# Cross-attention of a two-part layer rebuilt: half-array scores, merged value products, late softmax division, unrolled steps

## The chip, the cores and the metric

The kernel runs on one core of a Trainium2 chip. The metric is the device time of one execution in microseconds (us). The core has four compute engines that run their own instruction streams: PE (TensorE, matrix products; its weight loads are listed as PEld), DVE (VectorE), ACT (ScalarE) and POOL (GpSimd). SP (SyncE) only issues transfers. The streams wait for each other through semaphores.

## The reference

```python
x = x + xattn(layernorm(x), ctx, ctx, gamma)      # x, ctx: (4, 512, 512)
x = x + ffn(layernorm(x))
# xattn: 8 heads of 64 rows per batch, queries = rows of layernorm(x)
qk  = einsum('bhdq,bhdl->bhql', qh, kh) / sqrt(64)
ret = einsum('bhql,bhdl->bhdq', softmax(qk), vh)   # keys and values are both ctx
# ffn: shared part silu(x @ sw_gate) * (x @ sw_up) @ sw_down, times sigmoid(x @ shared_gate_w),
#      plus the two best of 8 experts of each row, by softmax(x @ router_w.T)
```

Everything is float32. The kernel reaches that precision by splitting each operand into a rounded high part and the low rest, and by adding the products high x high, high x low and low x high.

## The kernel before

The 2048 rows of x are 16 tiles of 128 rows; a tile holds two heads of 64 rows, called s = 0 and s = 1. The kernel has three stages: attention with the second norm and the router's logits, tile by tile; the shared part of the FFN, for four blocks of 512 rows and eleven weight chunks; and the routed experts, 39 slots of 128 rows. Only the first stage and its two ends are touched.

For one tile the attention stage does this. SP loads the tile of x twice (`xb` for the norm, `x2b` for the residual), the context rows once as `cn` for the values and once more, by half tiles, as `cd`, in which each head's 64 rows stand in both halves of the partitions. DVE takes the moments of `xb`, POOL the power -1/2 (`power`), ACT writes the normed queries `xn`. A query stationary `qs` holds, for one head, the high part in 64 partitions and the low part in the other 64 (ACT `queries_hi`, POOL `queries_lo`). POOL splits the keys into `kh` and `kl` (128x1024 each). PE's `scores` makes a 128x512 block of scores with two matmuls over all 128 rows (L1231, L1232), eight blocks a tile. DVE takes the negative row maximum (L922), ACT the exponential with its row sum (L679), DVE the reciprocal, POOL divides the block (`norm_p`, L548). PE transposes the probabilities (`probs_T`, L1239, 4 transposes of 128x128 into one bank), ACT copies the high part (`probs_hi`, L685), DVE subtracts for the low part (`probs_lo`, L931), and PE multiplies with the values in three matmuls of 512 columns (`times_v`, L1252, L1253, L1255) into `bO`. DVE's `rows_out` (L937) adds gamma times `bO` to `x2b`. Then follow the second norm (`moments`, `power`, ACT `normed`, giving `x2n`), a transposition (`rows_T`), its copy `x2T`, and `logits`. SP stores `x2b`, `x2n` and `x2T`.

The order of each engine's stream is written by hand in five functions `tile(t, i, par)`, run by `over_tiles` (L284): two pairs of tiles unrolled, a hardware loop, the last pair unrolled. Scores of tile t+1 are made between the products of tile t; the second norm of tile t-1 and the logits of t-2 ride along. Four banks hold scores, two (`bT`) transposed probabilities, one (`bO`) the product, one (`bM`) everything else.

At the far end the first two weight chunks of the shared part are split (`weights_hi`, `weights_lo`) within the last tile, and `tokens_hi`, `tokens_lo` split the first block of tokens there. PE runs `gate_up` for chunks 0 and 1 before the first `down`. The load of chunk 2 stands in SP's stream behind `store_columns` of the last tile; the splits of chunks 2 and later stand ahead of the first `hidden_hi` on ACT.

## Time and profile before

| | us |
|---|---|
| median of 3 runs | 939.79 (939.73 to 942.89) |
| the profiled execution | 942.02, span 939.7 |
| granted TensorE clock over the span | 0.980 |
| PE busy | 876.7 (93%) |
| DVE, ACT, POOL busy | 571.4, 518.9, 473.7 |
| attention stage, first instruction to the first matmul of the shared part | 0 to 278.2 |

An engine's busy time is the sum of its instructions' spans. Matmuls overlap each other in these spans, so what one costs is read from start to start. "Idle before, releaser" names what ended an engine's wait. Granted clock 1.00 means 2.4 GHz, 0.5 would be 1.2 GHz.

### The profile page before, as it was taken

What the parts mean: (1) busy time and instruction counts of PE and PEld (TensorE: products, weight loads), DVE (VectorE), ACT (ScalarE), POOL (GpSimd) and SP (SyncE); (2) the same over time, 40 slices, a digit from 0 to 9 for tenths busy, and PEclk for the clock granted to TensorE, in tenths of its full rate; (3) what the DMA queues carried; (4) which work ended last, traced back from release to release, by engine and by line L of the source; (5) the groups of instructions that cost most, each with busy time, mean ns of one, the idle gap of its engine ahead of it and who ended that gap; (6) DMA issues with size and microseconds to landing.
All of it is one profiled execution on the core that took longest, in us unless ns stands there. A gap on an engine that the chain in (4) does not pass through costs nothing.

```text
span 939.7 us, 14497 instructions
## 1 busy us (share of the span) xinstructions
PE 876.7 (93%) x4560; PEld 748.0 (80%) x4560; DVE 571.4 (61%) x920; ACT 518.9 (55%) x879; POOL 473.7 (50%) x460
## 2 busy tenths in 40 slices
PE   4899999899988999998899999999999999999993
PEld 3677777787767888886688888888899999999992
DVE  5788787878773642431121212112899999999892
ACT  4788888888765331120111211112688888888881
POOL 5787878787720000047100000000489999999984
PEclk9999999999999999999799999999999999999997
DMA  9344343525625322200032002552964444443542
GB/s 145 83 142 128 127 142 101 160 96 156 224 90 157 100 68 90 90 1 1 1 120 39 1 1 90 185 184 93 300 145 72 87 70 80 76 87 67 90 63 39
DMA packets 70142, 93.77 MB, mean 100 GB/s; under 512 B 16137, under 2 KB 35593, under 8 KB 70098
## 3 DMA queue, kind: packets, MB, share of 16 engines
q1 hardware_dynamic: 60338, 72.73, 25.9%
q0 software_dynamic: 9760, 20.49, 12.3%
q8 instruction: 24, 0.39, 0.2%
q14 instruction: 20, 0.16, 0.1%
HBM read 65.59 MB, written 27.60 MB: 99 GB/s over the span
## 4 chain that ended last, share of the span: by engine, by line
PE 68%; ACT 1%; issue 1%; DVE 1%; DMA 0%; POOLq 0%; SPq 0%; POOL 0%; DVEq 0%; ACTq 0%
PE bank L1347 9%; PE bank L1345 8%; PE bank L1346 8%; PE bank L1412 5%; PE bank L1414 5%; PE bank L1413 5%; PE bank L1359 4%; PE bank L1360 4%; PE bank L1361 4%; PE bank L1436 3%; PE bank L1437 3%; PE bank L1438 3%; PE bank L1369 2%; PE bank L1423 1%; DMA stg<-in_L_ffn_sw_down 0%
## 5 line engine op out<-in xcount | busy, mean ns | idle before, releaser
L1033 DVE TENSOR_TENSOR sg<-bank,sg 128x512 f32<-128x512 f32 x44 | 30.4, 692 | 224.0 <-PE bank L1347 187.5
L606 POOL DMA_INDIRECT xg<-x_normed_rows,meta x39 | 39.7, 1018 | 219.3 <-PE bank L1369 159.7
L1347 PE MATMUL bank<-x_hl,wsp 128*128 128x512 f32 x352 | 138.5, 393 | 5.2 <-issue 5.1
L1346 PE MATMUL bank<-x_hl,wsp 128*128 128x512 f32 x352 | 138.1, 392 | 2.3 <-issue 2.3
L1345 PE MATMUL bank<-x_hl,wsp 128*128 128x512 f32 x352 | 138.3, 393 | 0.7 <-issue 0.6
L785 ACT ACTIVATE sg<-bank 128x512 f32<-128x512 f32 x44 | 26.3, 597 | 164.9 <-PE bank L1347 147.8
L591 POOL DMA_INDIRECT slot_rows<-msrc,posi x32 | 32.9, 1030 | 135.9 <-DVE posi L1140 126.5
L685 ACT ACTIVATE pth<-bank 128x512 fp32r<-128x512 f32 x128 | 73.3, 598 | 45.8 <-PE bank L1239 43.9
L931 DVE TENSOR_TENSOR ptl<-bank,pth 128x512 fp32r<-128x512 f32 x128 | 86.0, 682 | 17.6 <-ACT pth L685 17.2
L792 ACT ACTIVATE hh<-sg 128x512 fp32r<-128x512 f32 x44 | 27.8, 631 | 123.7 <-DVE sg L1033 107.9
L548 POOL TENSOR_SCALAR pb<-pb,rinv 128x512 f32<-128x512 f32 x128 | 87.4, 696 | 13.3 <-DVE rinv L927 7.8
L679 ACT ACTIVATE pb<-bank,negmax 128x512 f32<-128x512 f32 x128 | 86.7, 688 | 0.7 <-DVE negmax L922 0.3
L922 DVE TENSOR_REDUCE negmax<-bank 128x1 f32<-128x512 f32 x128 | 81.9, 681 | 0.7 <-PE bank L1232 0.2
L1347 PEld LDWEIGHTS bank<-x_hl,wsp 128*128 128x128 f32 x352 | 66.7, 189 | 19.2 <-issue 5.4
L1345 PEld LDWEIGHTS bank<-x_hl,wsp 128*128 128x128 f32 x352 | 66.7, 189 | 17.6 <-issue 4.0
L617 POOL DMA_INDIRECT out<-y,meta x39 | 73.5, 1885 | 12.3 <-issue 5.5
L1346 PEld LDWEIGHTS bank<-x_hl,wsp 128*128 128x128 f32 x352 | 66.7, 190 | 15.2 <-issue 1.6
L1231 PE MATMUL bank<-kh,qs 128*128 128x512 f32 x128 | 57.7, 451 | 20.5 <-POOL qs L531 17.2
L627 POOL TENSOR_TENSOR wd<-wex,wd 96x512 fp32r<-96x512 f32 x39 | 74.5, 1911 | 3.3
L1239 PE MATMUL bank<-ident,pb 128*128 128x128 f32 x512 | 71.9, 273 | 4.2 <-POOL pb L548 4.2
L1239 PEld LDWEIGHTS bank<-ident,pb 128*128 128x128 f32 x512 | 61.3, 141 | 15.6 <-POOL pb L548 5.3
L1359 PE MATMUL bank<-wsp,hh 128*128 128x512 f32 x176 | 69.6, 395 | 2.9 <-DVE hl L1035 2.4
(157 smaller groups left out, 2353.9 us busy)
## 6 DMA issues: line engine op xcount, KB each, us to landing
cd<-in_ctx SPq DMA_DIRECT2D x32, 256.0 KB, 5.0
wex<-in_L_ffn_w_gate SPq DMA_DIRECT2D x8, 704.0 KB, 4.3
wex<-in_L_ffn_w_up SPq DMA_DIRECT2D x8, 704.0 KB, 5.7
xb<-in_x SPq DMA_DIRECT2D x16, 256.0 KB, 4.5
cn<-in_ctx SPq DMA_DIRECT2D x16, 256.0 KB, 3.0
x2b<-in_x SPq DMA_DIRECT2D x16, 256.0 KB, 2.8
x_rows<-x2b SPq DMA_DIRECT2D x16, 256.0 KB, 2.1
x_normed_rows<-x2n SPq DMA_DIRECT2D x16, 256.0 KB, 2.0
```

Source lines behind the costliest of these rows:

```text
L548: gp.tensor_scalar(pb[s][:, q, :], pb[s][:, q, :], rinv[:, s, q:q + 1], 0.0, ALU.mult, ALU.add).then_inc(g_pn, 1)
L617: g.indirect_dma_start(out=out, out_offset=bass.IndirectOffsetOnAxis(ap=meta[:, s, 0:1], axis=0), in_=y3[s % 2][:, :], in_offset=None, com ...
L627: gp.tensor_tensor(wd3[0:IR, 1, c], wex[0:IR, e, 2 * W3 + (IC - 1) * H:EW], wd3[0:IR, 0, c].bitcast(F32), ALU.subtract).then_inc(g_wd, 1)
L679: sc.activation(pb[s][:, q, :], bS[q][:, :], ACT.Exp, bias=negmax[:, s, q:q + 1], scale=1.0, accum_out=rsum[:, s, q:q + 1]).then_inc(a_exp, 1)
L685: sc.activation(pth[c][:, :], bT[c % 2][:, :], ACT.Copy).then_inc(a_pth, 1)
L922: ve.tensor_reduce(negmax[:, s, q:q + 1], bS[q][:, :], AX_X, ALU.max, negate=True).then_inc(d_max, 1)
L931: ve.tensor_tensor(ptl[c][:, :], bT[c % 2][:, :], pth[c][:, :].bitcast(F32), ALU.subtract).then_inc(d_ptl, 1)
L1239: ins = te.transpose(bT[c % 2][:, q * P:(q + 1) * P], pb[s][:, q, c * P:(c + 1) * P], ident[:, :])
L1345: te.matmul(bk[:, :], hi, xhi, start=(h == 0), stop=False)
L1346: te.matmul(bk[:, :], hi, xlo, start=False, stop=False)
L1347: ins = te.matmul(bk[:, :], lo, xhi, start=False, stop=(h == HC - 1))
L1359: te.matmul(bY[tt][:, :], th, hi, start=(c == 0), stop=False)
```

## The change

The work is the same up to the order of the operations. These parts change:

1. Loads: `cd` is gone; keys and values both come from `cn` (`load_keys` removed, one 256 KB load a tile where there were three).
2. Scores: `qh`, `ql`, `kh`, `kl` are 128x512 with one head in each half of the partitions. For each of the four 128-query chunks of a tile PE issues six matmuls of 64 rows by 512 columns, alternating between the halves of the array and between two banks. DVE takes the maxima of both heads of a chunk in one instruction of 2x512 elements.
3. Values: the stationary of a head is its 64 high and 64 low columns side by side, so the product with `pth` and with `ptl` takes two matmuls, not three, and leaves the high and the low contribution in the two halves of `bO`. ACT copies one half (`low_half`), DVE adds it to the other (`halves`), once a head.
4. The softmax division leaves `norm_p`. One reciprocal of eight sums a tile, spread by POOL to 128x512 (`spread`), transposed by PE (`inverses`), copied by ACT times gamma (`rgam`), multiplied into the product by POOL (`scaled`), and added to `x2b` by POOL (`residual`).
5. POOL now writes `xn`, `qh` and `x2n`; ACT's `normed` and `queries_hi` are gone.
6. Transposed probabilities rotate over three banks (`bT`, order `P_BANK`); the third also takes what `bM` took.
7. `over_tiles` runs `step(i)` for i from -3 to 20, fully unrolled. Step i has scores 1 to 3 of tile i and score 0 of tile i+1, transposes of tile i-1 (and the first of tile i), products of tiles i-1 and i-2, norm of tile i-3. On PE `gate_up(0, 0)` stands after step 16 and `gate_up(0, 1)` after step 17. SP issues in step i: `store_rows(i-4)`, `load_x2(i-2)`, `store_columns(i-5)`, `store_normed(i-5)`, `load_x(i+3)`, `load_values(i+1)`.

The core of the diff:

```diff
-        cd = [place(f"cd{j}", [P, 2, L]) for j in range(2)]
-        kh = [place(f"kh{j}", [P, 2, L], F32R) for j in range(2)]
-        qs = [place(f"qs{j}", [P, L], F32R) for j in range(2)]
-        vs = [place(f"vs{j}", [P, 2, LC, 3, DH], F32R) for j in range(2)]
+        kh = [place(f"kh{j}", [P, L], F32R) for j in range(2)]
+        qh = [place(f"qh{j}", [P, L], F32R) for j in range(2)]
+        vs = [place(f"vs{j}", [P, LC, 4, DH], F32R) for j in range(2)]
...
-        bS, bT, bO, bM = bank[0:4], bank[4:6], bank[6], bank[7]
+        bO, bT = bank[4], bank[5:8]
+        P_BANK = (2, 0, 2, 0, 2, 0, 1, 0)
...
+            def load_values(t):
+                after(sp, e_vt, t - 1)
                 after(sp, kl_done, t - 1)
+                sp.dma_start(cn[t % 2][:, :], c_t[t, :, :]).then_inc(ld_cn[t % 2], 16)
+
+            def load_x2(t):
+                after(sp, g_x2n, t - 1)
+                after(sp, st_x2[t % 2], 16 * (t // 2))
+                sp.dma_start(x2b[t % 2][:, :], x_t[t, :, :]).then_inc(ld_x2[t % 2], 16)
...
+            def spread(t):
+
+                g.wait_ge(d_rinv, t + 1)
+                after(g, e_R, t)
+                gp.tensor_copy(rspr[:, :, :], rinv[:, :, :].rearrange("p c s -> p (c s)").unsqueeze(2).to_broadcast([P, 2 * QC, DH])).then_inc(g_rspr, 1)
+
+            def scaled(t):
+
+                g.wait_ge(d_att, 2 * t + 2)
+                g.wait_ge(a_Rg, t + 1)
+                gp.tensor_tensor(att[t % 2][:, :], att[t % 2][:, :], rgam[:, :], ALU.mult).then_inc(g_att, 1)
...
+            def step(i):
+                if there(i + 1):
+                    keys_hi(i + 1)
+                    queries_lo(i + 1)
+                if there(i - 2):
+                    scaled(i - 2)
+                if there(i + 1):
+                    keys_lo(i + 1)
...
+                    shift(0, i + 2)
+                    queries(i + 2)
+                if there(i - 3):
+                    shift(1, i - 3)
+                if there(i + 2):
+                    queries_hi(i + 2)
+                if there(i - 3):
+                    rows_normed(i - 3)
+                if there(i - 2):
+                    residual(i - 2)
...
+                after(pe, a_exp, 8 * t + 2 * c - 2)
+                terms = ((qh, kh), (qh, kl), (ql, kh))
+                for n, (a, b) in enumerate(terms):
+                    for s in range(2):
+                        r = slice(DH * s, DH * (s + 1))
+                        ins = te.matmul(bSS[c % 2][:, s, :], a[t % 2][r, c * P:(c + 1) * P], b[t % 2][r, :], start=(n == 0), stop=(n == 2))
+                        if n == 2:
+                            ins.then_inc(e_s, 1)
...
-                te.matmul(bO[:, :], hi, pth[c][:, :], start=first, stop=False)
-                te.matmul(bO[:, :], lo, pth[c][:, :], start=False, stop=False)
-                pe.wait_ge(d_ptl, 4 * k + c + 1)
-                te.matmul(bO[:, :], hi, ptl[c][:, :], start=False, stop=last).then_inc(e_pv, 1)
...
+                te.matmul(bO[:, :], v, pth[n % 4][:, :], start=(c == 0), stop=False)
+                pe.wait_ge(d_ptl, 8 * t + n + 1)
+                te.matmul(bO[:, :], v, ptl[n % 4][:, :], start=False, stop=(c == LC - 1)).then_inc(e_pv, 1)
```

SP's stream, the transfers of one tile. First before (rows of the hardware loop; `cd` are the key halves, `st_`, `ld_` semaphores count landed transfers, `a_`, `d_`, `g_`, `e_` those of ACT, DVE, POOL, PE):

```order
L362 DMA x_normed_transposed<-x2T_100 128x512 [waits a_x2T]
L356 DMA x_rows<-x2b_95 128x512
L358 DMA x_normed_rows<-x2n_97 128x512 [waits a_x2n]
L352 DMA x2b_95<-in_x 128x512 [waits st_x20,a_x2n]
L344 DMA cn_72<-in_ctx 128x512 [waits e_vt]
```

And the same place in the change, one step:

```order
L351 DMA x_rows<-x2b_102 128x512 [waits g_x2]
L347 DMA x2b_102<-in_x 128x512 [waits st_x21,g_x2n]
L359 DMA x_normed_transposed<-x2T_105 128x512 [waits a_x2T]
L355 DMA x_normed_rows<-x2n_103 128x512 [waits g_x2n]
L337 DMA xb_69<-in_x 128x512 [waits d_stat0,g_xn]
L342 DMA cn_71<-in_ctx 128x512 [waits kl_done,e_vt]
```

The context load `cn`, of which the keys are now made as well, stands behind the load of `x2b`, which waits for POOL's `g_x2n`; before, the keys came by the loads `cd`, ahead of the stores.

POOL's stream in the change, one step (`att` is the product, `rgam` the spread inverse sums):

```order
L531 CAST kh_74<-cn_72 128x512 [waits e_s,ld_cn1]
L525 TENSOR_TENSOR ql_80<-xn,qh_78 128x512 [waits g_qh]
L554 TENSOR_TENSOR att_97<-att_97,rgam 128x512 [waits a_Rg,d_att]
L535 TENSOR_TENSOR kl_76<-cn_72,kh_74 128x512 [waits g_kh]
L504 TENSOR_TENSOR rstd<-vare,mhalf 128x1 [waits d_vare1]
L548 COPY rspr<-rinv 128x512 [waits e_R,d_rinv]
L504 TENSOR_TENSOR rstd<-vare,mhalf 128x1 [waits d_vare0]
L508 TENSOR_SCALAR nmr<-aggr,rstd 128x1 [waits g_rstd0]
L514 TENSOR_SCALAR xn<-xb_69,rstd,nmr 128x512 [waits g_nmr0]
L508 TENSOR_SCALAR nmr<-aggr,rstd 128x1 [waits g_rstd1]
L520 CAST qh_77<-xn 128x512 [waits e_s,g_xn]
L542 TENSOR_SCALAR x2n_104<-x2b_102,rstd,nmr 128x512 [waits e_x2T,st_x2n1,g_nmr1]
```

Eight divisions a tile have left this stream; three passes over the product, the normed rows and the spread sums have come in. The first row of a step waits for `cn`, and its last one here sets `g_x2n`.

PE's stream around one chunk of scores, before and in the change:

```order
L1239 MATMUL bank<-ident,pb_86 128x128 x3
L1231 MATMUL bank<-kh_75,qs_82 128x512 [waits a_exp]
L1232 MATMUL bank<-kl_77,qs_82 128x512
L1231 MATMUL bank<-kh_75,qs_82 128x512
L1232 MATMUL bank<-kl_77,qs_82 128x512
L1252 MATMUL bank<-pth_89,vs_84 128x512 [waits a_pth]
```

```order
L1214 MATMUL bank<-ident,pb_87 128x128 x3
L1205 MATMUL scores<-kh_74,qh_78 128x512 [waits a_exp,kl_done,ql_done]
L1205 MATMUL scores<-kh_74,qh_78 128x512
L1205 MATMUL scores<-kl_76,qh_78 128x512 x2
L1205 MATMUL scores<-kh_74,ql_80 128x512 x2
L1214 MATMUL bank<-ident,pb_87 128x128 [waits d_ptl]
```

Four matmuls for two score blocks became six for two blocks, each of half the rows; the wait for the keys (`kl_done`) sits on the first chunk of each tile.

## Rows read from the trace of the kernel before

**Rows 1.** One line, L937, the end of each tile (length ns, first and last start us)

```profile
L937 DVE SCALAR_TENSOR_TENSOR x2b<-bank,gam,x2b x16: 742/742/746, 39.5 to 278.6; 128x512 f32<-128x512 f32 x16
```

**Rows 2.** Busy us (x instructions) from 100 to 220: PE, PEld, DVE, ACT, POOL; PEclk, DMA

```profile
100.00:220.00 120.00, 109.98 (x651) 92.15 (x650) 97.32 (x210) 100.25 (x231) 94.53 (x118) 1.00 0.42 136
```

**Rows 3.** The timeline of PE, 15 to 17 us (start, length, instruction)

```profile
15.83 0.40 PE L1231 MATMUL bank<-kh,qs 128*128 128x512 f32 x1
16.07 0.39 PE L1232 MATMUL bank<-kl,qs 128*128 128x512 f32 x1
16.38 0.41 PE L1290 MATMUL bank<-ident,rg 9*128 9x9 f32 x4
16.72 0.50 PE L1231 MATMUL bank<-kh,qs 128*128 128x512 f32 x1
```

**Rows 4.** The timeline of PE, 123 to 127 us

```profile
123.80 0.95 PE L1279 MATMUL bank<-rgT,x2T 128*128 128x9 f32 x8
124.61 0.48 PE L1252 MATMUL bank<-pth,vs 128*128 128x512 f32 x1
...
126.07 1.03 PE L1239 MATMUL bank<-ident,pb 128*128 128x128 f32 x8
126.86 0.48 PE L1231 MATMUL bank<-kh,qs 128*128 128x512 f32 x1
```

**Rows 5.** The timeline of DVE, 121 to 124 us

```profile
121.53 1.25 DVE L922 TENSOR_REDUCE negmax<-bank 128x1 f32<-128x512 f32 x2
...
122.77 0.68 DVE L931 TENSOR_TENSOR ptl<-bank,pth 128x512 fp32r<-128x512 f32 x1
123.36 0.68 DVE L894 BATCH_NORM_STATS2 stats<-xb 128x6 f32<-128x512 f32 x1
```

**Rows 6.** The timeline of SP, the first and fifth transfer of a burst

```profile
65.37 0.33 SPq L358 DMA_DIRECT2D x_normed_rows<-x2n  x1
...
67.20 1.25 SPq L340 DMA_DIRECT2D cd<-in_ctx  x2
```

**Rows 7.** DMA issues from 145 to 153 us, a burst of six (last column: us to landing)

```profile
cd<-in_ctx SPq DMA_DIRECT2D x2, 256.0 KB, 4.3
...
cn<-in_ctx SPq DMA_DIRECT2D x1, 256.0 KB, 3.0
```

**Rows 8.** One line, L625, a cast on POOL (length min/median/max)

```profile
L625 POOL CAST wd<-wex x39: 601/1312/2017, 661.2 to 921.5; 96x512 fp32r x38, 96x512 fp32r<-96x512 f32 x1
```

**Rows 9.** Groups of instructions on POOL, 100 to 220 us (busy, mean ns, idle before)

```profile
L548 POOL TENSOR_SCALAR pb<-pb,rinv 128x512 f32<-128x512 f32 x60 | 41.0, 698 | 4.1 <-POOL qs L531 4.1
...
L542 POOL TENSOR_TENSOR kl<-cd,kh 128x1024 fp32r<-128x1024 f32 x7 | 16.8, 2399 | 0.0
...
L519 POOL TENSOR_TENSOR rstd<-vare,mhalf 128x1 f32<-128x1 f32 x14 | 7.7, 552 | 1.5 <-issue 1.5
L521 POOL TENSOR_SCALAR nmr<-aggr,rstd 128x1 f32<-128x1 f32 x14 | 3.7, 265 | 2.4 <-POOL rstd L519 2.4
```

**Rows 10.** The timeline of all engines at the start

```profile
8.77 7.43 SPq L335 DMA_DIRECT2D xb<-in_x  x1
...
20.62 1.35 PE L1239 MATMUL bank<-ident,pb 128*128 128x128 f32 x8 [2.70 <-POOL pb L548]
```

**Rows 11.** The timeline of all engines, 262 to 285 us

```profile
262.77 1.03 PE L1239 MATMUL bank<-ident,pb 128*128 128x128 f32 x8
...
267.52 1.91 ACT L714 ACTIVATE x_hl<-x_hl 128x2048 fp32r<-128x2048 f32 x1
...
269.46 2.29 DVE L972 TENSOR_TENSOR x_hl<-x_hl 128x2048 fp32r<-128x2048 f32 x1 [1.11 <-ACT x_hl L714]
...
274.63 1.75 DVE L966 TENSOR_TENSOR wsp<-stg,wsp 128x1536 fp32r<-128x1536 f32 x1
...
284.97 0.33 SPq L362 DMA_DIRECT2D x_normed_transposed<-x2T  x1
```

**Rows 12.** The timeline of PE at 294 us

```profile
294.01 0.47 PE L1359 MATMUL bank<-wsp,hh 128*128 128x512 f32 x1 [2.36 <-DVE hl L1035]
```

More of the change, by code:

```diff
@@ L1020, in _, with step @@
-            over_tiles(dve, tile)
-            rows_out(NT - 1, NI - 1, 1)
-            dve.wait_ge(d_x2, NT)
-            moments(1, NT - 1, x2b[1][:, :])
-            aggregate(1, NT - 1)
-            variance(1, NT - 1)
+            def step(i):
+                if there(i - 1):
+                    inverse(i - 1)
+                if there(i - 2):
+                    probs_lo(i - 2, 7)
+                if i == 1:
+                    router_columns()
+                if there(i - 1):
+                    values_lo(i - 1)
+                if there(i + 2):
+                    aggregate(0, i + 2)
+                if there(i - 1):
+                    probs_lo(i - 1, 0)
+                if there(i + 2):
+                    variance(0, i + 2)
+                if i == NT:
+                    weights_lo(0)
+                if there(i):
+                    maxima(i, 1)
+                if there(i - 1):
+                    probs_lo(i - 1, 1)
+                if there(i - 2):
+                    halves(i - 2, 1)
+                if there(i - 1):
+                    probs_lo(i - 1, 2)
+                if there(i - 3):
+                    second_norm(i - 3)
+                if there(i - 1):
+                    probs_lo(i - 1, 3)
+                if there(i - 3):
+                    aggregate(1, i - 3)
+                if i == NT:
+                    weights_lo(1)
+                if there(i):
+                    maxima(i, 2)
+                if there(i - 3):
+                    variance(1, i - 3)
+                if there(i - 1):
+                    probs_lo(i - 1, 4)
+                if there(i + 3):
+                    first_norm(i + 3)
+                if there(i):
+                    maxima(i, 3)
+                if there(i - 1):
+                    probs_lo(i - 1, 5)
+                    halves(i - 1, 0)
+                    probs_lo(i - 1, 6)
+                if i == NT - 1:
+                    tokens_lo(0, 0)
+                if there(i + 1):
+                    maxima(i + 1, 0)
@@ L1392, in block2 @@
                     rows3(1, 0, 1)
-            logits(NT - 2, 0)
+            for i in range(-3, NT + 1):
+                step(i)
             gate_up(0, 0, 0)
-            rows_T(NT - 1, 1)
-            logits(NT - 1, 1)
+            step(NT + 1)
+            gate_up(0, 1, 0)
+            for i in range(NT + 2, NT + 5):
+                step(i)
             for b in range(NB):
```

713 lines of the change are left out of this document (309 added, 404 removed).

## The prediction

> **What bounds the kernel now.** I read the page's slices first: PE is busy in nearly all of them, and only the first 278 us hold the work that changes. The end of a tile, L937, comes 16 times from 39.5 to 278.6 us, so a tile takes 239.1 / 15 = 15.94 us [rows 1]. Per tile the engines are busy, from 120 us in the middle [rows 2], PE 14.6, ACT 13.3, DVE 12.9, POOL 12.6 us. PE is nearest to the period, at clock 1.00 (2.4 GHz), and the missing 1.3 us are waits. What it does, from start to start: a matmul of 512 columns 0.24 us, alone or behind its like [rows 3]; the eight passes of the logits 0.81 us [rows 4]. Forty matmuls and ten blocks of four transposes then leave (14.6 - 40 x 0.235 - 0.8) / 10 = 0.44 us for a block; the bare spacing of eight is 0.79 us [rows 4].
>
> **PE after the change.** Values: 16 instead of 24 matmuls, 3.8 us. Eleven blocks of transposes (one is new, the inverse sums): 4.8. Logits: 0.8. Scores: 24 matmuls of half the rows. If the two of a pair run beside each other, 12 x 0.235 = 2.8 us; if not, 5.6. No row shows a 64-row matmul. They use different halves of the array and write different banks, and the weight loads that they need, one per matmul, are no more than what PE takes in transposes every 0.10 us [rows 4]; I take 2.8 and keep 5.6 as the other end. Four times a step PE goes into such a group and out again. The nearest row is the nine-row transposes: 16.07 to 16.38 us is 0.07 more than the usual 0.24 [rows 3], so eight changes cost up to 0.6 us. Sum: 12.8 us, against 14.6; the other end is 15.0 to 15.6.
>
> The Trainium skill, "TensorEngine Tiling (Array Packing)", Key Properties, says that tiles work in parallel but that a change of tiling mode drains the engine. By that rule, with a drain as the 0.16 us by which a matmul's length exceeds its spacing (0.39 against 0.235), the eight changes would cost 1.3 us and PE would stand at 13.5; the row shows half of that. Neither sum reaches the loop below; the rule would only lift rival B.
>
> **DVE.** A 512-wide pass costs 0.59 us, two maxima and a variance 1.24 [rows 5]. Four double maxima at 1.12 (a second 512 elements without a second start), eight `probs_lo`, the value split, two moments, two `halves` and 0.4 for small ones: 4.5 + 4.7 + 0.6 + 1.2 + 1.2 + 0.4 = 12.6 us. It hardly changes. **ACT** loses four passes (`xn`, `x2n`, two of `queries_hi`) and gets three; it stays under DVE. Reading the four streams beside each other with these lengths, every wait among PE, ACT and DVE closes within about 13.0 us, so DVE would set the pace.
>
> **POOL and SP: a new loop.** This is what I expect to decide. In step i SP may issue `load_x2(i-2)` only when POOL has finished `rows_normed(i-4)`; two stores, `xb`, and then `cn` stand behind it in SP's stream. `keys_hi`, POOL's first instruction of step i, waits for that `cn`, and `rows_normed(i-3)` is POOL's last but one in the same step. So one step closes one round: from the end of `x2n` to the issue of `cn`, its landing, and POOL's stream up to the next `x2n`. Before, the keys' loads were not behind `x2n` of the same round, since `cd` was issued a tile earlier.
> - Issue: the fifth transfer of a burst starts 1.83 us after the first [rows 6], plus 0.1 to wake.
> - Landing: 3.0 us for the third transfer of a burst, 4.3 for the fifth and sixth [rows 7]. Ours is the fifth of smaller ones: 3.8, bounds 3.0 and 4.3.
> - POOL: a cast of 512 at 0.57 (0.60 long at its shortest [rows 8]), three times with `spread`; three two-input passes at half of the 1024-wide 2.4 [rows 9], 3.6; two powers 1.1; two shifts 0.54, two waits on its own results at 2.4 / 14 = 0.17; a scaling at 0.67 and one at 0.70 [rows 9]. Sum 1.71 + 3.6 + 1.1 + 0.54 + 0.34 + 1.37 = 8.7 us. `residual` falls into the transfer's time.
>
> Together 1.9 + 3.8 + 8.7 = **14.4 us a step** (13.6 to 14.9), above 12.8 and 13.0. The saving of PE's 1.8 us is thus mostly handed back as a wait for the keys at `scores(i+1, 0)`, and nothing of it depends on PE's exact sum below 14.4.
>
> **The beginning.** PE's first transposes of probabilities start at 20.62 us now [rows 10]. In the change SP issues `cn` of tile 0 only behind `load_x(2)`, which waits for `queries(0)` on POOL, an estimate of 6.4 us. `cn` of tile 1 stands behind the table of slot rows, behind which SP's next issue now takes 7.43 us, from 8.77 to 16.2 [rows 10]. So it is issued at 17, lands at 20.5, and with cast, low queries and low keys (3.0) the scores of tile 1 start at 24; PE's stream has them ahead of the first transposes, which come at 26.4 us: 6 us later than now. Steps 1 to 3 do not close the loop yet and lack some products: 37.5 us, step 4 begins at 64. The keys of step 4 are ready 9.4 into it (`x2n(0)` ends 0.5 before it, then 1.9 + 3.8, a cast and three two-input passes), ten rounds of 14.4 follow, and 2.7 us of PE work: step 15 begins at 64 + 9.4 + 144 + 2.7 = 220.
>
> **The far end.** Now PE goes from the transposes of tile 15 at 262.77 to its first `down` at 294.01 us [rows 11, 12]: 31.2 us. In the change the chain is longer. From the start of step 15: 11 until `probs_lo(14, 6)`, 1.7 for the transposed values and two copies, 1.9 for `tokens_hi` (267.52), 2.3 for `tokens_lo` (269.46) on DVE, for which `probs_lo(14, 7)` and all behind it wait; then DVE, ACT and PE alternate through step 16 with two weight splits on each of ACT and DVE, 1.75 a piece there (274.63), inside it [rows 11]: the last product before `gate_up(0, 0)` ends 33.8 us after the start of step 15. `gate_up(0, 0)` is 24 x 0.235 = 5.6; the three products left 1.4. Then one dependent chain: half copied 0.7, `halves` 0.7, `scaled` 1.2, POOL's norm of tile 14 1.9, `residual` 1.25, moments to variance 1.2, power and shift 1.0, `x2n` 0.8, transposes and copy 1.3, and some hops: 10.9 us, where `x2b` to `x2T` took 6.4 before. From the store of the last `x2T` (284.97) to `down` it is 9.0 us, the load and split of chunk 2 [rows 11, 12]; SP's order there is unchanged. Sum 33.8 + 5.6 + 1.4 + 10.9 + 9.0 = 60.7. `gate_up(0, 1)` is covered. So `down` starts at 220 + 61 = 281 us, 13 us sooner than at 294. Everything behind it is the same program: unchanged, also the unrolled code (2903 listed PE rows against 2694).
>
> **Sum.** The profiled execution took 942.0 us, 2.2 above the median. 942.0 - 13 = 929; against the median 939.8 - 13 = **927 us**.
>
> **Rivals.**
> - B, the loop does not bind. `cn` lands in 3.0 us or the burst has thinned out, and DVE sets 13.0 to 13.3 us. For it: the loop's lower bound is 13.6, and the change moves six transfers of 256 KB a tile where eight are moved now, so that each may land sooner. Then 64 + 11 x 13.2 + 61 = 270, 24 us gained: 916 us.
> - C, slower: the two halves of a pair run one after the other. The nearest rows for it are that every matmul, whatever its rows, starts 0.235 after the last. PE then has 15.3 us a step: 26.4 + 14 x 15.3 - 1.5 + 61 = 300, 6 us later than now: 945.5 us. It decides from 14.9 us a step on, where the longer ends have eaten the gain.
> - D, POOL's passes are longer beside DVE: in the expert stage the cast of L625 takes 1.31 us at the median, 0.60 at its shortest [rows 8]. Against it: in this stage the 1024-wide pass takes a steady 2.40 with DVE busy 97 of 120 us [rows 2, 9], and DVE keeps reading banks. With a fifth more the loop is 16.1: step 15 at 237, `down` at 298, 4 us later than now: 944 us. The Trainium skill, "GPSIMD Engine Reference", Architecture, says that POOL's read and write ports are shared with DVE; by that rule, the long casts are such collisions.
>
> **How the numbers follow.** A measurement can tell about 0.5%, 4.7 us, from no change. My forecast has 0.50, B 0.22, C 0.13, D and mishaps at the ends 0.15. With 4 us of spread on each: faster 0.46 + 0.22 + 0.03 = 0.71; within 0.5% 0.04 + 0.06 + 0.08 = 0.18; slower 0.11. The range reaches from a little below B to C: 913 to 946 us.
>
> **What would show it.** Right: in the middle PE waits at the first scores of each tile for POOL's low keys, POOL waits some 4 us a step for `cn`, and the writes of `x2b` come every 14.4 us; the matmuls of the scores start 0.12 us apart on average; first transposes of probabilities at 26, the first `down` at 281, behind a wait of nearly 9 us. Wrong: PE without waits at 15 us a step (C), POOL passes beyond 1.3 us for 512 elements (D), or DVE without idle time (B). If the loop is right but the start or the end is not, the error shows in those two times alone.

## The result and the profile after

The changed kernel takes 950.23 us (median of 4, 949.24 to 951.39) and the one before, measured between its runs, 941.34 (939.73 to 943.52): ratio 1.0103, 95% interval 1.0078 to 1.0127. It is slower by about 1%, where 927 us (913 to 946) was forecast. Its profiled execution took 949.24, with a span of 947.5 us.

The page after: busy time of the engines, then the granted clock in 40 slices.

```profile
PE 869.6 (92%) x4624; PEld 718.8 (76%) x4624; DVE 569.3 (60%) x820; ACT 507.1 (54%) x863; POOL 428.6 (45%) x414
...
PEclk9899999989877999999799999999999999999997
```

The same stretch as [rows 2], 100 to 220 us, in the changed kernel (the same columns):

```profile
100.00:220.00 120.00, 109.02 (x696) 81.16 (x694) 98.40 (x164) 96.51 (x227) 73.99 (x98) 0.94 0.41 125
```

PE is busy 109.0 of 120 us, as before, although its work of a tile was meant to have shrunk. POOL has 20 us more of idle time, DVE and ACT stand about as before, and the clock has fallen from 1.00 to 0.94. The table of waits, 60 to 220 us (total us, times, longest us):

```profile
POOL kh L531 <- DMA cn<-in_ctx: 53.9, 10, 6.1
...
PE scores L1205 <- issue: 11.0, 7, 2.3
```

The longest wait is the forecast one, POOL's for `cn`: 5.4 us a time. One round of the loop shows in SP's and POOL's timelines:

```profile
129.61 0.33 SPq L347 DMA_DIRECT2D x2b<-in_x  x1
129.99 0.42 SPq L359 DMA_DIRECT2D x_normed_transposed<-x2T  x1
130.46 0.42 SPq L355 DMA_DIRECT2D x_normed_rows<-x2n  x1
130.99 0.43 SPq L337 DMA_DIRECT2D xb<-in_x  x1
131.51 0.41 SPq L342 DMA_DIRECT2D cn<-in_ctx  x1
131.97 0.45 SPq L351 DMA_DIRECT2D x_rows<-x2b  x1
```

```profile
120.91 0.61 POOL L531 CAST kh<-cn 128x512 fp32r<-128x512 f32 x1 [6.08 <-DMA cn<-in_ctx]
...
123.94 1.27 POOL L535 TENSOR_TENSOR kl<-cn,kh 128x512 fp32r<-128x512 f32 x1
...
128.81 0.77 POOL L542 TENSOR_SCALAR x2n<-x2b,rstd,nmr 128x512 f32<-128x512 f32 x1
...
136.84 0.61 POOL L531 CAST kh<-cn 128x512 fp32r<-128x512 f32 x1 [6.00 <-DMA cn<-in_ctx]
```

`x2n` ends at 129.58, `load_x2` leaves at 129.61, and `cn`, fifth of six, 1.9 us behind it at 131.51; the cast of the keys starts at 136.84, 5.3 us later. POOL's part from cast to the end of `x2n` is 8.67 us. From 85.56 to 225.23 us `cn` is issued nine times more, so a step takes 139.67 / 9 = **15.52 us**, not 14.4. What PE makes of it (timeline, before and behind its wait for the keys):

```profile
120.14 0.50 PE L1205 MATMUL scores<-kh,qh 64*128 64x512 f32 x2
120.47 0.40 PE L1205 MATMUL scores<-kl,qh 64*128 64x512 f32 x2
120.71 0.39 PE L1205 MATMUL scores<-kh,ql 64*128 64x512 f32 x2
121.03 0.50 PE L1228 MATMUL bank<-pth,vs 128*128 128x512 f32 x1
```

```profile
125.31 0.80 PE L1205 MATMUL scores<-kh,qh 64*128 64x512 f32 x2 [2.32 <-issue]
125.87 0.66 PE L1205 MATMUL scores<-kl,qh 64*128 64x512 f32 x2
126.30 0.66 PE L1205 MATMUL scores<-kh,ql 64*128 64x512 f32 x2
```

The low keys `kl` are ready at 125.21, and the first scores of the tile start at 125.31: the wait that the profile puts down as "issue" is the one for the keys. Each row of L1205 is two matmuls; a pair takes 0.235 us from start to start, and the spacings around a change of shape are longer, 0.32 or 0.33. Behind the wait of 2.3 us a spacing is 0.43: from 125.3 to 127.0 us the granted clock is 0.50 (1.2 GHz), from 130 us on again 1.00 (2.4 GHz).

### The profile page after: what moved, and what is told of

It reads as the page before. It is cut to its first block, busy times and chain, and to the rows that moved or that the text cites. A ratio compares the mean times of both kernels' runs of the same rounds, so it can differ in the third digit from the quotient of the medians.

```text
span 947.5 us, 13669 instructions
## 1 busy us (share of the span) xinstructions
PE 869.6 (92%) x4624; PEld 718.8 (76%) x4624; DVE 569.3 (60%) x820; ACT 507.1 (54%) x863; POOL 428.6 (45%) x414
## 4 chain that ended last, share of the span: by engine, by line
PE 87%; issue 4%; DMA 3%; DVE 2%; ACT 2%; POOL 1%; SPq 0%; POOLq 0%; DVEq 0%; ACTq 0%
PE scores L1338 9%; PE scores L1337 9%; PE scores L1336 9%; PE bank L1214 6%; PE scores L1205 5%; PE bank L1350 4%; PE bank L1351 4%; PE bank L1352 4%; PE bank L1228 4%; PE bank L1230 3%; PE bank L1432 3%; PE bank L1433 3%; PE bank L1431 3%; PE scores L1407 3%; PE scores L1409 3%
## 5 line engine op out<-in xcount | busy, mean ns | idle before, releaser
L997 DVE TENSOR_TENSOR sg<-scores,sg 128x512 f32<-128x512 f32 x44 | 30.4, 692 | 224.3 <-PE scores L1338 187.5
L1338 PE MATMUL scores<-x_hl,wsp 128*128 128x512 f32 x352 | 139.4, 396 | 3.9 <-issue 3.7
L1337 PE MATMUL scores<-x_hl,wsp 128*128 128x512 f32 x352 | 138.9, 395 | 2.5 <-issue 2.4
L1336 PE MATMUL scores<-x_hl,wsp 128*128 128x512 f32 x352 | 139.3, 396 | 0.1
L768 ACT ACTIVATE sg<-scores 128x512 f32<-128x512 f32 x44 | 26.3, 597 | 165.9 <-PE scores L1338 144.8
L663 ACT ACTIVATE pb<-scores,negmax 128x512 f32<-128x512 f32 x128 | 87.8, 695 | 19.9 <-DVE negmax L905 19.7
L915 DVE TENSOR_TENSOR ptl<-bank,pth 128x512 fp32r<-128x512 f32 x128 | 86.5, 677 | 12.5 <-ACT pth L669 12.2
L1214 PE MATMUL bank<-ident,pb 128*128 128x128 f32 x512 | 83.2, 288 | 9.8 <-DVE ptl L915 9.2
L905 DVE TENSOR_REDUCE negmax<-scores 128x2 f32<-128x1024 f32 x64 | 77.4, 1210 | 20.9 <-PE scores L1205 20.8
L1338 PEld LDWEIGHTS scores<-x_hl,wsp 128*128 128x128 f32 x352 | 67.3, 191 | 22.2 <-issue 8.3
L1337 PEld LDWEIGHTS scores<-x_hl,wsp 128*128 128x128 f32 x352 | 67.4, 192 | 15.6 <-issue 1.8
L1336 PEld LDWEIGHTS scores<-x_hl,wsp 128*128 128x128 f32 x352 | 67.3, 191 | 14.7 <-issue 0.8
L620 POOL DMA_INDIRECT out<-y,meta x39 | 68.2, 1749 | 12.5 <-issue 5.2
L1113 DVE TENSOR_TENSOR wg<-wex,wg 128x1408 fp32r<-128x1408 f32 x39 | 63.4, 1626 | 12.1 <-ACT wg L794 12.1
L1352 PE MATMUL bank<-wsp,hl 128*128 128x512 f32 x176 | 69.4, 395 | 0.0
```

The source lines that it names most:

```text
L620: g.indirect_dma_start(out=out, out_offset=bass.IndirectOffsetOnAxis(ap=meta[:, s, 0:1], axis=0), in_=y3[s % 2][:, :], in_offset=None, com ...
L663: sc.activation(pb[t % 2][s][:, c, :], bSS[c % 2][:, s, :], ACT.Exp, bias=negmax[:, c, s:s + 1], scale=1.0, accum_out=rsum[:, c, s:s + 1]) ...
L905: ve.tensor_reduce(negmax[:, c, :], bSS[c % 2][:, :, :], AX_X, ALU.max, negate=True).then_inc(d_max, 1)
L915: ve.tensor_tensor(ptl[n % 4][:, :], bT[P_BANK[n]][:, :], pth[n % 4][:, :].bitcast(F32), ALU.subtract).then_inc(d_ptl, 1)
L1214: ins = te.transpose(bT[P_BANK[n]][:, q * P:(q + 1) * P], pb[t % 2][s][:, q, c * P:(c + 1) * P], ident[:, :])
L1336: te.matmul(bk[:, :], hi, xhi, start=(h == 0), stop=False)
```

## Three places, each moved by an experiment

The time of the first `down` product tells most of the run: before it came at 294.01 us [rows 12], and 645.7 us of span followed; after it comes at 303.49, and 644.0 follow. So the loss of 8 to 9 us lies in the part that I had summed, and every experiment can be read by that time. The kernels were measured on several chips, each beside the kernel before, which took 927 to 944 us there, so I compare ratios to before; step and first `down` come from each profile. The column of the first transposes scatters: all versions but those with the context early have the same SP stream up to them, and still differ by over 3 us.

| kernel | ratio to before (95%) | step, us | first transposes | first `down` |
|---|---|---|---|---|
| before | 1 | 15.9 | 20.62 | 294.01 |
| after | 1.0103 (1.0078 to 1.0127) | 15.5 | 30.67 | 303.49 |
| loads first | 0.9951 (0.9917 to 0.9986) | 13.62 | 31.39 | 288.88 |
| GpSimd order | 0.9941 (0.9910 to 0.9971) | 13.62 | 32.15 | 288.01 |
| keys twice | 1.0197 (1.0145 to 1.0249) | 16.1 | 35.74 | 314.91 |
| loads first, keys twice | 0.9959 (0.9934 to 0.9984) | 13.62 | 34.54 | 290.05 |
| loads first, `values_lo` twice | 0.9950 (0.9922 to 0.9978) | 13.62 | 34.38 | 290.75 |
| loads first, halves apart | 0.9958 (0.9940 to 0.9976) | 13.63 | 33.72 | 289.64 |
| context early | 1.0082 (1.0049 to 1.0115) | 15.5 | 28.94 | 301.42 |
| context early, slot rows later | 0.9991 (0.9960 to 1.0022) | 15.7 | 21.02 | 296.00 |
| gate and up later | 1.0125 (1.0044 to 1.0206) | 15.6 | 31.79 | 304.99 |
| loads first, splits spread | 0.9888 (0.9834 to 0.9941) | 13.62 | 34.89 | 288.17 |
| and the end rearranged | 0.9770 (0.9738 to 0.9801) | 13.62 | 34.43 | 276.97 |
| all, and the start | 0.9685 (0.9658 to 0.9711) | 13.62 | 22.48 | 265.25 |

### The middle: is the loop the bound?

**Loads first.** `load_x` and `load_values` go to the head of SP's step:

```
             def step(i):
+                if there(i + 3): load_x(i + 3)
+                if there(i + 1): load_values(i + 1)
                 if there(i - 4): store_rows(i - 4)
                 if there(i - 2): load_x2(i - 2)
                 if there(i - 5): store_columns(i - 5); store_normed(i - 5)
-                if there(i + 3): load_x(i + 3)
-                if there(i + 1): load_values(i + 1)
```

> Edit: in each step SP issues load_x and load_values first, then the stores and load_x2 that wait for POOL. Theory (the loop x2n -> load_x2 -> cn -> keys -> x2n sets the period of the changed kernel, 15.5 us a step from the issue of one cn to the next): the loop is cut, the steps come every 13.0 to 13.5 us (DVE is next), POOL no longer waits for cn in the middle, and with some eleven rounds the time falls by 22 to 28 us against the changed kernel, to 922 to 928 us. Rival 1 (the transfers are slow by themselves, the order does not matter): within 3 us of the changed kernel. Rival 2 (PE is the bound, its groups of half-array matmuls cost more than they look): steps stay above 15 us, POOL's waits turn into waits for PE.

Measured: 936.02 us, 14 us under the changed kernel by the ratios. The busy times show what bounds now:

```profile
100.00:220.00 120.00, 120.00 (x815) 89.73 (x814) 112.52 (x189) 111.90 (x264) 86.57 (x113) 1.00 0.44 137
```

PE has not one idle interval, and the clock is 1.00. POOL still waits for `cn`, 29.8 us in 12 rounds instead of 53.9 in 10, but nothing that PE needs waits with it. The gain is less than the 22 to 28 us expected: the step stops at 13.62, not at 13.0 to 13.5, and not eleven rounds get shorter but some nine, since the first wait behind the loop ends 16.7 us sooner (239.19 instead of 255.88). The landing of `cn` also fell, by the table of DMA issues, 60 to 220 us (median us to landing), first after, then here:

```profile
cn<-in_ctx SPq DMA_DIRECT2D x10, 256.0 KB, 4.7
```

```profile
cn<-in_ctx SPq DMA_DIRECT2D x11, 256.0 KB, 2.9
```

So the landing was long in the burst, six transfers within 2.4 us, and is short here, where the loads are spread over the step. The next version stands between them: six transfers within 3.7 us, and 3.7 us to landing.

**GpSimd order.** The second, independent cut leaves SP alone and lets `x2n` end earlier on POOL:

```
                 if there(i + 2): inverse_deviation(0, i + 2)
+                if there(i - 3): shift(1, i - 3); rows_normed(i - 3)
                 if there(i + 2): shift(0, i + 2); queries(i + 2)
-                if there(i - 3): shift(1, i - 3)
                 if there(i + 2): queries_hi(i + 2)
-                if there(i - 3): rows_normed(i - 3)
                 if there(i - 2): residual(i - 2)
```

> Edit: on POOL shift(1) and rows_normed(i-3) stand ahead of the power, shift, queries and queries_hi of tile i+2, so 2.6 us less of POOL's work lies between the arrival of cn and x2n; SP's order is unchanged. Theory (the loop): 15.5 - 2.6 = 12.9, so the DVE takes over at 13.0 to 13.5 us a step and the time falls by 20 to 27 us, about as with SP's order changed, though nothing of the transfers is touched. Rival (the transfers themselves limit, some 6 us of them per step behind one another): the time falls by under 5 us.

Measured: 935.28 us, the step again 13.62. Two edits with nothing in common but the loop give 14 and 15 us.

**Keys twice**, on the changed kernel and on the version with the loads first:

```
+                gp.tensor_copy(kh[t % 2], cn[t % 2]).then_inc(g_kh0, 1)
+                g.wait_ge(g_kh0, t + 1)
                 gp.tensor_copy(kh[t % 2], cn[t % 2]).then_inc(g_kh, 1)
```

> The changed kernel with the cast of the keys done twice on GpSimd (0.6 us more a tile, between the landing of cn and everything behind it). Theory A (the loop x2n, load of x2, two stores, xb, cn, landing, GpSimd work to the next x2n sets the step from step 4 on): eleven rounds longer by 0.6 to 0.7 us each and 1 to 2 us at the start, +8 us, 957 to 960. Rival B (the steps are long because TensorE or VectorE is, or because of transfers in common): GpSimd has 4 us of idle time a step, +1 to +2 us for the start alone, 951 to 952.

> The same doubled cast on top of the version whose loads stand at the head of SyncE's step (936.0). Theory A: there the loop is cut and TensorE sets the step at 13.6 us, GpSimd's waits for cn take up the 0.6 us, only the start gets 1 to 2 us longer: 937 to 938. Rival B (GpSimd's work is still on the path): 8 us more, 944.

Measured: +0.0094 of the ratio on the changed kernel, 8.9 us, and the step from 15.52 to 16.10 by these issues of SP (144.88 us in nine steps); on the other +0.0008, 0.8 us, step 13.62. The same pass costs a step its 0.58 us in the one and nothing in the other. The loop is shown. The first `down` of the slow one moved by 11.4 us, more than the loop gives, because its start is 5.1 us late: 1 us is the doubled pass, the rest the scatter explained under "The start".

```profile
75.88 0.38 SPq L343 DMA_DIRECT2D cn<-in_ctx  x1
...
220.76 0.43 SPq L343 DMA_DIRECT2D cn<-in_ctx  x1
```

**`values_lo` twice**, with the loads first, asks whether PE or DVE stops the step at 13.62:

```
+                ve.tensor_tensor(vs_lo, bT[1], vs_hi, ALU.subtract).then_inc(d_vl0, 1)
+                dve.wait_ge(d_vl0, t + 1)
                 ve.tensor_tensor(vs_lo, bT[1], vs_hi, ALU.subtract).then_inc(d_vl, 1)
```

> The version with the loads first (step 13.62 us), with VectorE's pass for the low part of the values done twice, 0.6 to 0.7 us more of VectorE a step, which is then busy 13.4 of 13.62 us. Theory A: what bounds this version is TensorE, by the spacing of its products (a step between the two shapes of the array costs 0.09 us, and each first product with a new stationary behind another 0.32 instead of 0.235), which makes 13.6 us where the prediction summed 12.8: the step stays within 0.2 us of 13.62, +0 to +3 us in all. Rival B (VectorE's in-order queue is the bound, whatever its gaps): +0.6 to +0.7 us a step, 14.2 to 14.3, +9 to +11 us in all.

```profile
100.00:220.00 120.00, 120.00 (x810) 89.33 (x809) 117.91 (x201) 111.78 (x264) 86.20 (x112) 1.00 0.43 139
```

Measured: DVE goes from 112.5 to 117.9 busy us of 120, and neither step nor ratio moves. VectorE is not the bound, and TensorE, without an idle interval, is. Its timeline (loads first, one group of a chunk):

```profile
124.92 0.47 PE L1228 MATMUL bank<-pth,vs 128*128 128x512 f32 x1
125.23 0.40 PE L1230 MATMUL bank<-ptl,vs 128*128 128x512 f32 x1
125.56 0.50 PE L1205 MATMUL scores<-kh,qh 64*128 64x512 f32 x2
125.89 0.40 PE L1205 MATMUL scores<-kl,qh 64*128 64x512 f32 x2
126.12 0.39 PE L1205 MATMUL scores<-kh,ql 64*128 64x512 f32 x2
126.44 0.50 PE L1228 MATMUL bank<-pth,vs 128*128 128x512 f32 x1
126.78 0.40 PE L1230 MATMUL bank<-ptl,vs 128*128 128x512 f32 x1
```

A change of shape stretches two spacings, not one. Into the group it is 125.23 to 125.89, 0.66 us where two spacings are 0.47; out of it 126.12 to 126.78, again 0.66. Over the eight steps from 97.5 to 206.5 us the 32 entries cost 0.19 us more than the plain spacings on average, the 32 exits 0.17. Eight changes a step are 1.4 us, and that is the difference: 28 products and pairs at 0.235, 44 transposes of 128x128 at 0.109 and eight passes of the logits at 0.112 are 12.3 us, and the step is 13.6. My reading ahead of that run, 0.09 us a change and the rest in the first products of the values, was wrong. Those products do take 0.31 us to the next start behind a block of transposes (124.92 to 125.23), but they start 0.03 us behind the last transpose instead of 0.11, so the sum is the plain one. The kernel before has the same:

```profile
127.18 0.40 PE L1232 MATMUL bank<-kl,qs 128*128 128x512 f32 x1
```

Eight transposes from 126.07 [rows 4] at 0.109 and one product at 0.235 lead to 127.18, though the product starts at 126.86.

### The pairs in the array

**Halves apart**, with the loads first: the three products of one half of the rows, then the three of the other.

```
-                for n, (a, b) in enumerate(terms):
-                    for s in range(2):
+                for s in range(2):
+                    for n, (a, b) in enumerate(terms):
```

> The version with the loads first (936.0, step 13.62 us, TensorE busy without a gap), with the score products of one head's half of the rows issued three in a row, and then those of the other half, instead of in pairs. Theory A: neighbours in the two halves of the array run side by side (two products in 0.235 us), and apart they run one after the other: twelve times 0.235 less one overlap at each of the four changes of half, 1.9 to 2.8 us more a step, 15.5 to 16.4 us, sixteen steps: +28 to +45 us, 964 to 981. Rival C (each product of 64 rows takes half the time by itself, in whatever order): 936 to 938, no change.

Measured: no change, against theory A, but not for rival C's reason either. The timeline of PE:

```profile
124.45 0.51 PE L1205 MATMUL scores<-kh,qh 64*128 64x512 f32 x2
124.79 0.40 PE L1205 MATMUL scores<-kl,qh 64*128 64x512 f32 x2
125.03 0.40 PE L1205 MATMUL scores<-kh,ql 64*128 64x512 f32 x2
```

Starts are recorded, also where ends are modelled. In the program all three products of the first half stand ahead of the second half's first; in the trace both halves' `kh,qh` start before either's `kl,qh`. So the second half's first product started ahead of two that stand before it in the program: here each half of the array worked through its own three products, and the order between the halves did not matter. The Trainium skill, "TensorEngine Tiling (Array Packing)", Key Properties, says that tiles operate independently and can load weights and multiply in parallel; this trace agrees, and adds that adjacency in the program is not needed. It also says that a change of mode drains the engine; here a change costs 0.17 to 0.19 us, close to the 0.16 that I had worked out for that rule, and I had put 0.07 into the sum.

### The start

**Context early**: `cn` of tiles 0 and 1 is loaded right behind `xb` of tiles 0 and 1.

```
+                if i == -2: load_values(0); load_values(1)
-                if there(i + 1):
+                if i > 0 and there(i + 1):
                     load_values(i + 1)
```

> Edit: cn of tiles 0 and 1 is loaded right behind xb of tiles 0 and 1, ahead of the small loads and the table of slot rows. Theory (the late start is the position of these two loads): PE's first transposes of probabilities come at 20 to 22 us instead of 30.7, and the whole time falls by 8 to 10 us against the changed kernel; the middle keeps its 15.5 us a step. Rival (the loop's phase swallows an earlier start, since its first round waits for x2n of tile 0 anyway): the first transposes come earlier, but the time falls by under 3 us.

Measured: 948.75 us, 2 us gained by the ratios, whose intervals overlap, where 8 to 10 were expected. The first transposes came at 28.94 instead of 30.67: something else was late. The table of DMA issues of this run, 0 to 30 us, names it (KB each, median us to landing):

```profile
slot_rows<-meta SPq DMA_DIRECT2D x1, 39.0 KB, 16.8
```

The table of slot rows is 39 KB, but leaves in pieces of 8 bytes and lands 16.8 us later. In the changed kernel `cn` of tile 1, issued at 15.16, stood behind it and POOL waited for it (POOL's timeline):

```profile
24.50 0.62 POOL L531 CAST kh<-cn 128x512 fp32r<-128x512 f32 x1 [9.07 <-DMA cn<-in_ctx]
```

Here `xb` of tile 3, issued at 12.04, landed at 26.2, and VectorE's first pass over it holds the maxima behind it. The landing of the slot rows also explains the scatter of the starts. It took 14.6 us in the changed kernel, and 15.3 to 18.9 in the seven other versions with this start; in all eight the first transposes come 16.0 to 16.3 us behind that time (14.6 and 30.67, 15.3 and 31.39, 18.9 and 34.89), and 17.0 in the two with the keys twice.

**Context early, slot rows later**: the same, and the store moved behind the loads of the dense part's third block.

```
-                sp.dma_start(meta_d..., meta...).then_inc(st_meta0, 16)
...
             load_block(2, 0)
+            sp.wait_ge(g_const, N_CONST)
+            sp.dma_start(meta_d..., meta...).then_inc(st_meta0, 16)
             store_out(0)
```

> The second cut of the start: as in the run with the first two context tiles loaded early, and the store of slot_rows (39 KB in pieces of 8 bytes, 16.8 us from issue to landing there, while xb of tile 2, issued 3.0 us behind it, landed at 26.2 us) moved to the place behind the loads of block 2's columns in the dense part. Theory A: those small pieces stand ahead of every later transfer of the queue, so moving them lets xb and cn through in 3 to 5 us, first transposes of probabilities near 21 us instead of 28.9, and the whole run 7 to 10 us below the changed kernel, 940 to 943. Rival B: the start is set by the chain of norm, scores and exponentials, and the small pieces cost nothing: 948 to 949, as with the early context tiles alone.

Measured: ratio 0.9991, 10.5 us under the changed kernel, first transposes at 21.02. The first `down` moved by 7.5 us, since the loop in the middle is still there. The rest of the run is as long as before (644.4 us behind the first `down`), so the store costs nothing in its new place. The store was not moved by itself.

### The end

**Gate and up later**:

```
-            gate_up(0, 0, 0)
             step(NT + 1)
+            gate_up(0, 0, 0)
             gate_up(0, 1, 0)
```

> Edit: on PE step 17 stands ahead of gate_up(0, 0), not behind it. Theory (gate_up(0, 0), 7.0 us, delays the last three value products and with them the whole chain to the last x2T and to the load of chunk 2): that chain starts 6 to 7 us sooner, both gate_up still lie inside it, and the time falls by 5 to 7 us. Rival (the chain is not what ends the wait of the first down; the weights or tokens are): the time moves by under 2 us.

Measured: nothing gained (ratio 1.0125, interval over that of the changed kernel). The last value product ended earlier, but its successor did not start earlier:

```profile
287.68 0.77 POOL L542 TENSOR_SCALAR x2n<-x2b,rstd,nmr 128x512 f32<-128x512 f32 x1
```

```profile
293.42 0.60 PE L1248 MATMUL bank<-ident,x2n 128*128 128x128 f32 x4
```

The last `x2n`, tile 15's, is ready at 288.45, but its transposes and those of tile 14 ahead of them stand behind `gate_up(0, 1)` until 293.42. In the changed kernel only `gate_up(0, 0)` held this chain up; `gate_up(0, 1)` ran beside the norm of tile 15, whose `x2n` was ready at 292.77, and ended at 292.3. Here both stand in a row between the chain and the last transposes, 5.5 to 7 us each, and what the move gained is lost again. Also untouched are the three waits that come first (the changed kernel's chain of waits):

```profile
252.86 2.29 DVE L936 TENSOR_TENSOR x_hl<-x_hl 128x2048 fp32r<-128x2048 f32 x1 [3.69 <-ACT x_hl L701]
...
261.59 1.76 DVE L930 TENSOR_TENSOR wsp<-stg,wsp 128x1536 fp32r<-128x1536 f32 x1 [4.57 <-ACT wsp L696]
...
271.11 1.76 DVE L930 TENSOR_TENSOR wsp<-stg,wsp 128x1536 fp32r<-128x1536 f32 x1 [4.42 <-ACT wsp L696]
```

DVE stands at a split until ACT has done its half, with `probs_lo` and so PE's next product behind it: PE waits 4.6, 4.5 and 3.1 us and works at half its clock behind each.

**Splits spread**, with the loads first: ACT's high parts stand two or three passes ahead of DVE's low parts, and the last pair a step later.

```
 ScalarE:
-                if i == NT: tokens_hi(0, 0)
                 if there(i): exps(i, 0, 0); exps(i, 0, 1)
...
                 if there(i - 1): probs_hi(i - 1, 2)
-                if i == NT: weights_hi(0)
+                if i == NT: tokens_hi(0, 0)
...
                 if there(i - 1): probs_hi(i - 1, 4); probs_hi(i - 1, 5)
-                if i == NT: weights_hi(1)
+                if i == NT: weights_hi(0)
...
                 if there(i - 1): probs_hi(i - 1, 7)
+                if i == NT + 1: weights_hi(1)
 VectorE:
-                if i == NT: weights_lo(0)
                 if there(i - 1): probs_lo(i - 1, 1)
...
-                if i == NT: weights_lo(1)
                 if there(i - 1): probs_lo(i - 1, 4)
+                if i == NT: tokens_lo(0, 0)
+                if i == NT + 1: weights_lo(1)
                 if there(i - 1): probs_lo(i - 1, 5); halves(i - 1, 0); probs_lo(i - 1, 6)
-                if i == NT - 1: tokens_lo(0, 0)
+                if i == NT: weights_lo(0)
```

> On top of the version with the loads first (936.0): the six passes that split the tokens and the first two weight chunks (ScalarE 1.9, 1.5, 1.5 us, VectorE 2.3, 1.75, 1.75 us) are moved out of the place where each VectorE pass waits for its ScalarE pass ahead of a pass that TensorE needs; they stand two or three passes later on VectorE than on ScalarE, and the last pair a step later. TensorE waited 4.6, 4.5 and 3.1 us for them and ran at half its clock behind each wait. Theory A: most of these 12 us are the in-order wait and go, the passes' own time stays in part: 7 to 11 us less, 925 to 929, the first down product at 278 to 282 instead of 288.9. Rival B: the two engines' work in the steps 16 and 17 is the bound whatever its order, or the end is set by the last stores and the load of the third chunk: 934 to 936.

```profile
244.43 0.66 PE L1214 MATMUL bank<-ident,pb 128*128 128x128 f32 x4 [1.16 <-DVE ptl L915]
...
248.65 0.66 PE L1214 MATMUL bank<-ident,pb 128*128 128x128 f32 x4 [1.40 <-DVE ptl L915]
...
252.00 0.77 PE L1336 MATMUL scores<-x_hl,wsp 128*128 128x512 f32 x1 [2.02 <-DVE wsp L930]
...
268.75 0.79 PE L1336 MATMUL scores<-x_hl,wsp 128*128 128x512 f32 x1 [4.54 <-DVE wsp L930]
...
288.17 0.76 PE L1350 MATMUL bank<-wsp,hh 128*128 128x512 f32 x1 [7.38 <-DVE hl L999]
```

Measured: the three waits fell from 12.2 to 1.2 + 1.4 + 2.0 us, and the last value product came at 260.96, about 7 us sooner. But the second gate and up product now waits 4.5 us for its weights, and the first `down` moved by 0.7 us only; the ratio fell by 0.006, 6 us, but the intervals overlap, and the spans of the profiles differ by 1.8. The start of this profile was 3.5 us later by the slot rows, so part of the gain is hidden there. How much this edit is worth by itself is not settled; of the 7 us gained at the last value product most was lost again to what stood behind, as the rival had it.

**The end rearranged**, on top:

```
 TensorE:
-            gate_up(0, 0, 0)
             step(NT + 1)
-            gate_up(0, 1, 0)
+            gate_up(0, 0, 0)
             for i in range(NT + 2, NT + 5): step(i)
+            gate_up(0, 1, 0)
 SyncE, at the end of its step:
+                if i == NT + 1: load_chunk(2)
+                if i == NT + 3: load_chunk(3)
...
-            for c in range(2, SC):
+            for c in range(4, SC):
                 load_chunk(c)
 ScalarE:
                 silu_hi(0, c)
+                if c == 0: hidden_hi(0, c)
                 if c + 2 < SC: weights_hi(c + 2)
-                hidden_hi(0, c)
+                if c > 0: hidden_hi(0, c)
```

> On top of the spread splits: the first gate and up product stands behind the last value products of tile 15 (in front of them it held up everything of the last tile for 7 us), the second one behind the last transposes and logits, the third and fourth weight chunks are loaded before the last stores, and ScalarE makes the high part of the first hidden block before it splits the third chunk. Theory A: the last value product then ends near 253 us, the chain of the last tile to its stores takes some 11 us and runs beside the two gate and up products (14 us), and the first down product starts at 268 to 273 instead of 288.2: 15 to 20 us less than with the splits alone, 913 to 918. Rival B: the gate and up products only change places with the last tile's work, and the first down product still waits for the stores and the third chunk: 4 us less at most, 928 or more.

Measured: ratio 0.9770, 0.012 or 11 us under the spread splits, and the first `down` at 276.97, 11.2 us sooner, where 15 to 20 were expected. This is why it stopped there:

```profile
272.82 1.28 ACT L772 ACT_TABLE_LOAD   x1 [4.82 <-DMA x_normed_rows<-x2n]
```

ACT still waits for the last store, which I had put behind the fourth chunk's three loads. Loading that chunk behind the stores was not tried.

**All**, with the start of the previous section:

> All cuts together: loads first, spread splits, the end rearranged, and the start of the run with slot_rows later. The start gave 10 us on the changed kernel (ratio to before 0.9991 against 1.0103). If start, middle and end are separate stretches of one chain, as theory A says, it gives 8 to 10 us here too: 904 to 910 us, ratio to before 0.960 to 0.967. If the middle takes up what the start gives (rival B: a fixed rate of transfers or of the steps from 60 us on decides when step 15 ends), it ends within 3 us of the version without the changed start.

Measured: 897.28 us where the kernel before took 926.86 on the same chip, ratio 0.9685 (0.9658 to 0.9711): 3% faster than before and 4% faster than the change, with the same arithmetic. Start, middle and end add up, since they are stretches of one chain: 0.0085 or 8 us from the start here too, and the first `down` at 265.25. The ratio is a little above the 0.960 to 0.967 expected, by what the end had not given.

## Why the prediction was wrong, step by step

The first `down` was put at 281 and came at 303.49 us. The 22.5 us divide by my own steps.

- **The loop (10 x 14.4)**: right in mechanism, wrong in one term. Issue 1.9 as put, POOL 8.7 as put, landing 4.7 at the median and 5.3 in the round shown, where I took 3.8 between 3.0 and 4.3 [rows 7]. I took it below the 4.3 of a burst of before "of smaller ones", while the transfers of that burst are the same 256 KB. The 4.3 was itself one burst; over 60 to 220 us the trace of before has the longer landing too:

```profile
cd<-in_ctx SPq DMA_DIRECT2D x20, 256.0 KB, 4.7
```

  Step 15 starts at 237.2 us, 206.5 behind the first transposes, where I had 193.6: 12.9 us, of which ten rounds of 1.1 are 11.
- **The start (26.4)**: 4.3 us late. I had seen that `cn` of tile 1 stands behind the slot rows, and gave it a landing of 3.5 us from its issue at 17. SP issued it at 15.16, sooner than that, but it landed with the slot rows, 9.3 us later. I had priced what they cost SP [rows 10] and not what they cost the transfers behind them.
- **The far end (60.7)**: 66.3 us. From the start of step 15 to `gate_up(0, 0)` 38.4 us against 33.8, and 7.0 for that product against 5.6. What I had not priced is in the changed kernel's chain of waits (start, length, what):

```profile
255.88 1.12 PE bank L1214 x4
256.99 0.43 PE bank L1228
...
264.01 1.11 PE bank L1214 x4
265.12 0.42 PE bank L1228
...
275.63 0.43 PE scores L1336
```

Behind each wait PE's products come 0.43 us apart, not 0.235. From 255.88 to 259.57 and from 264.01 to 268.53 PE works 8.2 us in this way, and half of that, some 4 us (an estimate from the two spacings), would not have been there at the upper level, 2.4 GHz; the first eight products of `gate_up(0, 0)` make the 1.4. The chain from the last value product to the last store took 10.9 us, as put, and 8.6 from there to `down` against 9.0.
- **Behind the first `down`**: unchanged, as put (644.0 against 645.7).
- **PE after the change (12.8)**: 13.6; no part of the miss in the middle, since the loop hid it, but it bounds every repair. The term that was too small is the eight changes of shape: 0.6 us in the sum, from one spacing before the transposes of nine rows, against 1.4 measured over both spacings of each change. The other estimate of the prediction, 1.3 and PE at 13.5, was the better one. That DVE would set the pace if the loop did not was wrong for the same reason. The pairs run side by side, as I took, and rival C was false. Rival D was false too: POOL's passes took 1.27 us. Rival B's state was reached only by cutting the loop, and then it was TensorE, not VectorE, that set the pace.

So the forecast of a gain of 13 us was a small difference of larger terms: some 33 us gained in the middle against 6 lost at the start and some 13 at the far end (estimates: by the 15.94 us of a tile [rows 1], the place of step 15 lies near 247 us in the kernel before). The gain was too large by 13, of which the landing is 11, and the losses too small by 10. Each of the three errors has the same sign, and each came from a price taken in a calmer place of the trace of before than the one where it was to be paid: a landing from one short burst, a landing from a queue without the slot rows ahead, a product at the full clock behind a wait. That all three went one way was not foreseen: the chance of 0.11 for slower had room for one of them.

## What to carry to other kernels

When a load is moved behind a wait in its queue's stream, follow the loop through landing and the engine that uses it to the next wait: if it closes once a step, it sets the step, and every 0.1 us in it counts once a tile, wherever it is. Put loads that depend on nothing ahead of the stores and of waits for late results, and price a landing by the burst in which the transfer will stand, not by the same transfer of before. At the seam between two stages look for passes in pairs on two in-order engines (one makes the high part, the other the low part): with two or three passes between the two halves PE's waits fell from 12.2 to 4.6 us here. And when products change the shape of the array, price the change over the spacing on either side of it.

## What the runs showed of the hardware

- A transfer of 39 KB in pieces of 8 bytes landed 14.6 us after its issue in the changed kernel and up to 18.9 in the others with the same start, and 256 KB in rows 2.9 us; the two of 256 KB that stood behind it in the queue landed with it, 9.3 and 9.5 us after their issue.
- 256 KB landed in 2.9 us at the median with the transfers spread over a step, in 3.7 with six within 3.7 us, and in 4.7 with six within 2.4 us.
- Two products of 64 rows in different halves of the array take the time of one, 0.235 us, both alternating and with three of one half ahead of three of the other in the program. A change between the two shapes costs 0.17 to 0.19 us, spread over two spacings: 1.4 us of each step of 13.6.
- TensorE's granted clock over 100 to 220 us was 0.94 with a wait of up to 2.3 us a step, and 1.00 without one; products behind such a wait came 0.43 us apart (the lower level, 1.2 GHz), those later 0.235 (2.4 GHz). By these spacings the two waits of 4.6 and 4.5 us at the far end cost TensorE some 4 us more than their own length (an estimate).
